# Scores of the middle stage from f16 halves instead of f32, with the context's halves kept in DRAM

## The chip, the core and the metric

The kernel runs on one core of one Trainium2 chip. A core has a matrix engine (PE, whose weight loads the profile shows apart as PEld), three engines for elementwise work (DVE, ACT and POOL), a sequencer that here only issues transfers (SP), and 16 DMA engines that move data between DRAM and on-chip memory. Each engine runs its own list of instructions in order, and engines wait for each other through semaphores. The metric is device microseconds (us) of one execution; less is better.

## What is computed

A small model over 32 batches: 112 query rows, 375 context rows, width 256. Cut to what matters:

```python
x = x + cross_attention_16_heads(ctx, layernorm(x))              # first stage
x = x + mixture_of_8_relu_experts(layernorm(x), counts_of_top2)  # first and middle stage
q = layernorm(x)                                                 # middle stage, "x2n"
logits = einsum('bqd,bkd->bqk', q, ctx) * 256**-0.5 + mask * -1e9
x = x + einsum('bqk,bkd->bqd', softmax(logits), ctx)
x = x + top2_of_8_experts(layernorm(x), W1, b1, W2, b2)          # routing in the middle stage, experts in the last
```

The change touches how `logits` is multiplied out.

## The kernel before

There are three stages, one after the other. The **first** (`attention_phase`, about the first half of the span) computes the 16-head attention batch by batch, with five batches in flight. For each batch SP loads the context transposed (`ctxT`, f32, 375 KB, line 244), ACT rounds it to f16 (`ctx_hi`, line 812), and POOL subtracts to get the rest (`ctx_lo`, f16, line 344). The key and value products then use three f16 products (high times high, high times low, low times high) in place of one f32 product. In the profile these tiles are all named `we`, since they lie in the memory of the later expert weights.

The **middle** stage (`middle_phase`) runs 39 steps. Step `u` works on several batches at once, as a pipeline with lags: the mixture of batch group `u` (`mixture`, 24 f16 matmuls of 448 columns, steps 0 to 31), the attention of batch `u-4` (called `a` in the code), its softmax and output (`o`, lag 5), the routing norm and logits (`r`, lag 6), and the choice of experts and scatter (`k`, lag 7). From step 7 on all parts are there; the mixture ends with step 31, and in steps 32 to 35 everything but the mixture runs. No scheduler orders this work: each engine has a function `step` in which its instructions stand in a written order, and semaphores do the rest. The lines that matter, by engine and in the order in which they stand in a step:

- PE: transposes of the mixture's sum (L1532), mixture parts 0 and 1 (L1516), transposes of `probs` (L1543), mixture part 2, the output product (L1551), transposes of `x2n` (L1557), mixture part 3, transposes of the routing row `rows` (L1564), two small rank products (L1575, L1576), **the scores** (L1582, two f32 products of 375 columns, each in two records), six route products (L1593).
- ACT: `probs` (L1621), `probsT` (L1626), `x2n` (L1632), `logit_exp` (L1636), `rows` (L1643), `w_hi` (L1649, the f16 rounding of a piece of the last stage's weights), `x2nT` (L1653), `xT_hi` (L1657).
- POOL: `ln_var`, `ln_rstd` and `ln_shift` for `x2n` (L1439, L1441, L1451), the same for `rows` (L1439, L1441, L1460), `mask_add` (L1466), `w_lo` (L1473, which waits for `w_hi` of the same step), a token number (L1480), and two scatters `dispatch_dram` (L1490, which wait for the slots that DVE writes on L1801).
- DVE: scores plus mask (L1713), norm statistics, four accumulations of the mixture (L1689, L1693), the choice of experts, `x3` (L1781, named `we` in the profile), `xT_lo` (L1788), rank pick and `slots_at` (L1797 to L1801).
- SP: a load of `w_raw`, of `ctxT` (f32 again, 375 KB, for the scores), of the mask and of `ctx_rows` per batch, and the store of `x3`.

The **last** stage (`expert_phase`) runs 35 tiles of 256 tokens through the chosen experts. It isn't touched.

Of the kernel before, what the change touches and what calls it, by code (L numbers as in the profile page):

```python
# [82 lines left out]
def attention_phase(nc, ctx, dram, keep):  # L83
# [14 lines left out]
    def within(cols, dt):  # L98
# [66 lines left out]
        x1n_ready x1lo_ready logits_ready choice_ready  # L165
# [67 lines left out]
    with nc.Block(no_gpsimd_drain=True) as block:  # L233

        @block.sync
        def _(sp):
            def load(t, u):
# [7 lines left out]
                             dram["ctxT"][bass.ds(b, 1), :, :].rearrange("o (c p) s -> p (o c) s", p=128)).then_inc(ctx_in[u % 2], 16)  # L245

# [19 lines left out]
            def step(t, u, on, more):  # L266
# [24 lines left out]
                if UNROLL <= t * UNROLL + u < B - 2:  # L291
                    load(t, u + 2)
                if a:
# [15 lines left out]
            for b in range(last - 2, last + 1):  # L309
# [18 lines left out]
        def _(pool):  # L328
# [467 lines left out]
        def _(act):  # L796
# [420 lines left out]
def middle_phase(nc, ctx, dram, keep):  # L1217
# [23 lines left out]
    ctxT = sb("ctxT2", [128, 2, DC, KV], F32)  # L1241
# [9 lines left out]
    x2nT = sb("x2nT", [128, DC, S], F32)  # L1251
# [20 lines left out]
    def reuse(*shape):  # L1272
# [42 lines left out]
    names = """weights_in bias_in share_ps share_rdy bias_rdy we_hi_rdy we_lo_rdy route_split consts  # L1315
        ctxT_in0 ctxT_in1 rows_in0 rows_in1 mask_in0 mask_in1 passed
        ffn_done accT_done x2nT_done s1_done pT_done o_done x3nT_done route_done
        x2nT_rdy exp_rdy pT_rdy x3hi_rdy lexp_rdy
        acc_rdy x2_rdy st2 ag2 x2n_rdy masked_rdy eb_rdy inv_rdy x3_rdy st3 ag3 x3n_rdy x3lo_rdy
        lg_rdy top_rdy at_rdy negtop_rdy pair_rdy sumw_rdy which_rdy comb_rdy chosen_rdy rank_done pick_rdy slots_rdy  # L1320
        cum_rdy token_rdy scattered0 scattered1 scattered2 scattered3 x3_out0 x3_out1 pads_out w_in0 w_in1 w_hi_rdy w_lo_rdy rows_set late_in tally_done table
# [42 lines left out]
    with nc.Block(no_gpsimd_drain=True) as block:  # L1364

        @block.sync
        def _(sp):
# [14 lines left out]
            for n in range(2):  # L1382
                sp.dma_start(dram["dispatch"][DUMMY + n * 128:DUMMY + (n + 1) * 128, :], dram["pads"][n]).then_inc(m["pads_out"], 16)
            for n in range(3):
                sp.dma_start(dram["out"][PAD_OUT + n * 128:PAD_OUT + (n + 1) * 128, :], dram["pads"][n][:, 0:D]).then_inc(m["pads_out"], 16)
# [7 lines left out]
            def load(t, u):  # L1393
# [6 lines left out]
                sp.dma_start(ctxT[:, p, :, :], dram["ctxT"][bass.ds(b, 1), :, :].rearrange("o (c p) s -> p (o c) s", p=128)).then_inc(ctxT_in[p], 16)  # L1400
# [20 lines left out]
            sp.wait_ge(m["pads_out"], 16 * 5)  # L1421
            sp.wait_ge(m["late_in"], 16 * len(keep["late_loads"]))
# [75 lines left out]
        def _(pe):  # L1498
# [4 lines left out]
            last.then_inc(m["share_ps"], 1)  # L1503
            pe.wait_ge(m["share_rdy"], 1)
# [16 lines left out]
            def step(t, u, on):  # L1521
# [38 lines left out]
                if r:  # L1560
                    wait(pe, m["x3n_rdy"], cnt(t, ur, 1, 1))
                    wait(pe, m["lg_rdy"], cnt(t, ur - 1, 1, 1))
                    for kc in range(DC):
                        last = nc.tensor.transpose(psum[:, 7, kc * S:(kc + 1) * S], rows[:, ur % ROW_SLOTS, kc * 128:(kc + 1) * 128], ident[0:S, 0:S])  # L1564
                    last.then_inc(m["x3nT_done"], 1)
                if k:
# [9 lines left out]
                    nc.tensor.matmul(rank, ones[:, 0:S], cum[:], start=False, stop=True).then_inc(m["rank_done"], 1)  # L1576
                if a:
# [3 lines left out]
                    for kc in range(DC):  # L1581
# [601 lines left out]
```

## Time and profile before

| | us |
|---|---|
| median of three runs (1086.59 to 1091.59) | 1090.93 |
| the profiled execution, its own time | 1090.87 |
| its span, first to last instruction | 1089.1 |
| PE busy in the span | 983.3 |
| DVE, POOL, ACT busy | 785.0, 560.8, 549.5 |
| middle stage, first mixture product to last scatter | 518.7 to about 844 |

A busy time is a sum over instructions. Matmul records overlap (each is drawn longer than the time to the next one's start), so a PE that looks busy all the time need not be what the others wait for. What a piece of work costs in a row of matmuls is read from start to start.

### The profile page before, as it was taken

How to read it: one execution, taken by the hardware profiler on the slowest of the kernel's cores; microseconds unless marked ns; L12 is line 12 of the kernel's file. 1: busy time of each engine (PE TensorE's matmuls, PEld its weight loads, DVE VectorE, ACT ScalarE, POOL GpSimd, SP SyncE). 2: the span in 40 equal slices, each digit the busy share in tenths (PEclk: the TensorE clock that was granted, in tenths of full speed). 3: DMA queues.
4: the chain of work that ended last, by engine and by line, in shares of the span. 5: the costliest groups of instructions: out<-in, count | busy, mean ns of one | idle time of the engine just before them, and what ended most of it. 6: DMA issues, size and time to landing. Idle time of an engine off the chain costs nothing. (4 is left out here: it accounts for less than half of the span.)

```text
span 1089.1 us, 31550 instructions
## 1 busy us (share of the span) xinstructions
PE 983.3 (90%) x10736; PEld 689.5 (63%) x10736; DVE 785.0 (72%) x2259; ACT 549.5 (50%) x1090; POOL 560.8 (51%) x839
## 2 busy tenths in 40 slices
PE   4699999999999999987999999999974599999993
PEld 3366666666666666655466666666643478888873
DVE  4578888888888888874768888888855256666653
ACT  3366666666666666653233344333432255555551
POOL 6545554555555555401146666666665245555444
PEclk9899999999999999987999999999987699999997
DMA  5444344443444444312545655565551345565543
GB/s 166 138 138 125 108 119 128 133 133 112 121 117 116 132 134 116 92 48 77 159 134 175 176 175 177 176 180 177 167 162 53 108 82 93 91 101 95 86 62 39
DMA packets 104589, 133.95 MB, mean 123 GB/s; under 512 B 23680, under 2 KB 93776, under 8 KB 104272
## 3 DMA queue, kind: packets, MB, share of 16 engines
q1 hardware_dynamic: 90898, 113.86, 36.2%
q0 software_dynamic: 13536, 18.10, 9.7%
q8 instruction: 89, 1.46, 0.6%
q14 instruction: 66, 0.54, 0.2%
HBM read 93.78 MB, written 38.68 MB: 122 GB/s over the span
## 5 line engine op out<-in xcount | busy, mean ns | idle before, releaser
L973 DVE TENSOR_REDUCE smax<-psum 112x2 f32<-112x750 f32 x240 | 221.3, 934 | 51.9 <-PE psum L425 48.8
L805 ACT ACTIVATE probsT<-psum 125x896 f32<-125x896 f32 x173 | 158.8, 918 | 59.2 <-PE psum L440 57.8
L1941 POOL DMA_INDIRECT out_dram<-y,token_at x70 | 110.8, 1583 | 117.3 <-DMA out_dram<-y,token_at 56.0
L2022 ACT ACTIVATE h<-psum,b 128x256 f32<-128x256 f32 x140 | 58.8, 471 | 105.6 <-PE psum L1969 105.6
L1490 POOL DMA_INDIRECT dispatch_dram<-rows,slots_at x64 | 64.2, 1003 | 45.7 <-DVE slots_at L1801 33.2
L1693 DVE SCALAR_TENSOR_TENSOR acc<-psum,neg_bias,acc 128x448 f32<-128x448 f32 x112 | 76.0, 680 | 11.8 <-PE psum L1516 11.6
L425 PE MATMUL psum<-k_stack,q_stack 63*128 63x375 f16 x480 | 79.0, 329 | 3.5 <-DVE smax L973 0.7
L460 PE MATMUL psum<-probsT,v_aug 125*32 125x112 f32 x2688 | 81.6, 262 | 0.0
L440 PE MATMUL psum<-q_stack,k_stack 64*128 64x112 f16 x1384 | 64.6, 213 | 11.9 <-DMA q_stack<-neg_max 7.7
L382 POOL CAST k_hi<-we 128x375 f16<-128x375 f32 x64 | 32.0, 500 | 79.0 <-ACT we L825 78.9
L1516 PE MATMUL psum<-xT_hi,we_hi 128*128 128x448 f16 x256 | 70.2, 356 | 1.9 <-DVE we_lo L1667 1.9
L1516 PE MATMUL psum<-xT_lo,we_hi 128*128 128x448 f16 x256 | 70.1, 356 | 0.0
L1516 PE MATMUL psum<-xT_hi,we_lo 128*128 128x448 f16 x256 | 69.9, 355 | 0.0
L440 PEld LDWEIGHTS psum<-q_stack,k_stack 64*128 64x128 f16 x1384 | 37.2, 95 | 50.6 <-ACT probsT L805 23.9
L460 PEld LDWEIGHTS psum<-probsT,v_aug 125*32 125x32 f32 x2688 | 61.6, 109 | 9.2 <-issue 4.8
L1969 PE MATMUL psum<-x_hi,w_hi 128*128 128x256 f16 x280 | 56.5, 284 | 11.0 <-DVE x_lo L2036 5.9
L493 PE MATMUL psum<-wv_hi,we 128*125 128x256 f16 x384 | 62.2, 285 | 1.5 <-ACT we L825 1.5
L384 POOL TENSOR_TENSOR k_lo<-we,k_hi 128x375 f16<-128x375 f32 x64 | 56.0, 876 | 5.1
L1621 ACT ACTIVATE probs<-probs,exp_bias 112x375 f32<-112x375 f32 x32 | 19.4, 607 | 77.1 <-DVE exp_bias L1716 77.1
L1969 PE MATMUL psum<-x_lo,w_hi 128*128 128x256 f16 x280 | 55.8, 283 | 0.0
L1969 PE MATMUL psum<-x_hi,w_lo 128*128 128x256 f16 x280 | 55.7, 282 | 0.0
L476 PE MATMUL psum<-we,wk_hi 128*128 128x375 f16 x256 | 53.4, 332 | 2.5 <-ACT we L825 1.1
(276 smaller groups left out, 2506.1 us busy)
## 6 DMA issues: line engine op xcount, KB each, us to landing
k_stack<-k_hi_dram SPq DMA_DIRECT2D x64, 188.0 KB, 2.9
we<-in_ctxT_dram SPq DMA_DIRECT2D x32, 375.0 KB, 3.8
ctxT<-in_ctxT_dram SPq DMA_DIRECT2D x32, 375.0 KB, 5.1
ctx_rows<-in_ctx_dram SPq DMA_DIRECT2D x32, 375.0 KB
rows_e<-dispatch_dram SPq DMA_DIRECT2D x70, 136.0 KB
w_raw<-in_w_dram SPq DMA_DIRECT2D x32, 256.0 KB, 4.2
k_hi_dram<-k_hi SPq DMA_DIRECT2D x32, 188.0 KB, 2.2
k_lo_dram<-k_lo SPq DMA_DIRECT2D x32, 188.0 KB, 2.1
```

The lines of the kernel that those rows point to most:

```text
L425: last = nc.tensor.matmul(psum[:, pair_bank(s) + a, 0:KV], queries(rows, b4, s, 128), keys_at(rows, b4, s, 0, KV), start=True, stop=True)
L440: last = nc.tensor.matmul(psum[:, a, r * S:(r + 1) * S], keys_at(rows, b4, 4 * hg + r, c * KC, 128), queries(rows, b4, 4 * hg + r, S), sta ...
L460: last = nc.tensor.matmul(bank_d[32 * j:32 * j + 32, g * S:(g + 1) * S], v_aug[:, b4d, cc, h, :], probsT[:, b2d, cc, h // 8, h % 2, h // 2 ...
L493: last = nc.tensor.matmul(bank[0:KC, n * D:(n + 1) * D], x[:, b2a, kc, cc * KC:(cc + 1) * KC], w[:, kc, :], start=(done == 0), stop=(done ...
L805: nc.scalar.activation(probsT[:, p, c, hg, :, :, :].rearrange("p k h q -> p k (h q)"), psum[0:KC, 0:2, 0:4 * S], ACT.Exp, scale=float(HD) ...
L973: nc.vector.reduce_max(smax[:, (u - LAG_B) % 2, 2 * (s % 4) + s // 4::PAIRS], psum[0:S, pair_bank(s):pair_bank(s) + 2, 0:KV], AX.X).then_i ...
L1490: nc.gpsimd.indirect_dma_start(dram["dispatch"], bass.IndirectOffsetOnAxis(slots_at[:, uk % ROW_SLOTS, n:n + 1], 0), rows[:, uk % ROW_SLOT ...
L1516: last = nc.tensor.matmul(psum[:, mix_bank(t, u, k), 0:GT], w[:, kc, e, hc * 128:(hc + 1) * 128], x[:, kc, bass.ds(g0, GT)], start=(n == 0 ...
L1693: nc.vector.scalar_tensor_tensor(out, psum[:, mix_bank(t, u, k), 0:GT], neg_bias[:, hc, e:e + 1], out, ALU.max, ALU.add).then_inc(m["acc_r ...
L1941: nc.gpsimd.indirect_dma_start(dram["out"], bass.IndirectOffsetOnAxis(token_at[:, n % 2, s:s + 1], 0), y[:, n % 2, s, :], None, compute_op ...
L1969: last = nc.tensor.matmul(psum[:, 1 + c // 2, (c % 2) * TILE:(c % 2 + 1) * TILE], w[:, bass.ds(e, 1), kc, c * 128:(c + 1) * 128].rearrange ...
L2022: nc.scalar.activation(h[:, c, :], psum[:, 1 + c // 2, (c % 2) * TILE:(c % 2 + 1) * TILE], ACT.Relu, bias=b1[:, c, bass.ds(e, 1)]).then_in ...
```

## The change

In the first stage, SP stores both halves of each batch's context to a new DRAM tensor `ctx_halves`, and ACT and POOL wait until a buffer's halves are out before they overwrite it. In the middle stage, SP reads these halves (f16, twice 187.5 KB) in place of the f32 `ctxT` (375 KB), and the scores become six f16 products (three pairs of halves, two chunks each) in place of two f32 ones. ACT writes the high half of the transposed `x2n`, DVE a new low half. Three orders change: on ACT `x2nT_hi` goes ahead of `rows`, and `w_hi` to the step's end; on PE the routing transposes go behind the rank products. Two pairs of semaphores are merged.

```diff
+            def halves_out(b):
+
+                for n, half_of in enumerate((ctx_hi, ctx_lo)):
+                    sp.dma_start(dram["ctx_halves"][b, n, :, :], half_of[:, b % 2, :, :].rearrange("p c k -> p (c k)")).then_inc(m["ctx_out"], 16)
...
+                if b >= 2:
+                    halves_out(b - 2)
...
+                if t * UNROLL + u >= B - 2:
+                    wait(sp, m["ctxlo_ready"], count(t, u, 1, 1))
+                    apart(sp)
+                    halves_out(t * UNROLL + u)
...
+            sp.wait_ge(m["ctx_out"], 32 * B)
...
                 wait(pool, m["v_done"], count(t, u - 2, 2, 2))
+                wait(pool, m["ctx_out"], count(t, u - 2, 32, 32))
                 nc.gpsimd.tensor_tensor(ctx_lo[:, u % 2, :, :], ctxT[:, u % 2, :, :], ctx_hi[:, u % 2, :, :], ALU.subtract).then_inc(m["ctxlo_ready"], 1)
...
                 wait(act, m["v_done"], count(t, u - 2, 2, 2))
+                wait(act, m["ctx_out"], count(t, u - 2, 32, 32))
                 nc.scalar.activation(ctx_hi[:, u % 2, :, :], ctxT[:, u % 2, :, :], ACT.Copy).then_inc(m["ctxhi_ready"], 1)
...
-                sp.dma_start(ctxT[:, p, :, :], dram["ctxT"][bass.ds(b, 1), :, :].rearrange("o (c p) s -> p (o c) s", p=128)).then_inc(ctxT_in[p], 16)
+                sp.dma_start(ctx_halves[:, p, :, :, :].rearrange("p n c k -> p n (c k)"),
+                             dram["ctx_halves"][b, :, :, :].rearrange("n p f -> p n f")).then_inc(ctxT_in[p], 16)
...
                 mix(3)
-                if r:
-                    wait(pe, m["x3n_rdy"], cnt(t, ur, 1, 1))
-                    wait(pe, m["lg_rdy"], cnt(t, ur - 1, 1, 1))
-                    for kc in range(DC):
-                        last = nc.tensor.transpose(psum[:, 7, kc * S:(kc + 1) * S], rows[:, ur % ROW_SLOTS, kc * 128:(kc + 1) * 128], ident[0:S, 0:S])
-                    last.then_inc(m["x3nT_done"], 1)
                 if k:
...
                     nc.tensor.matmul(rank, ones[:, 0:S], cum[:], start=False, stop=True).then_inc(m["rank_done"], 1)
+                if r:
+                    wait(pe, m["x3n_rdy"], cnt(t, ur, 1, 1))
+                    wait(pe, m["lg_rdy"], cnt(t, ur - 1, 1, 1))
+                    for kc in range(DC):
+                        last = nc.tensor.transpose(psum[:, 7, kc * S:(kc + 1) * S], rows[:, ur % ROW_SLOTS, kc * 128:(kc + 1) * 128], ident[0:S, 0:S])
+                    last.then_inc(m["x3nT_done"], 1)
                 if a:
                     wait(pe, ctxT_in[ua % 2], loads(t, ua))
                     wait(pe, m["x2nT_rdy"], cnt(t, ua, 1, 1))
                     wait(pe, m["masked_rdy"], cnt(t, ua - 1, 1, 1))
-                    for kc in range(DC):
-                        last = nc.tensor.matmul(psum[0:S, 4, 0:KV], x2nT[:, kc, :], ctxT[:, ua % 2, kc, :], start=(kc == 0), stop=(kc == DC - 1))
+                    n = 0
+                    for x, half_of in ((x2nT_hi, 0), (x2nT_hi, 1), (x2nT_lo, 0)):
+                        if n == 2 * DC:
+                            wait(pe, m["x2lo_rdy"], cnt(t, ua, 1, 1))
+                        for kc in range(DC):
+                            last = nc.tensor.matmul(psum[0:S, 4, 0:KV], x[:, kc, :], ctx_halves[:, ua % 2, half_of, kc, :], start=(n == 0), stop=(n == 5))
+                            n += 1
                     last.then_inc(m["s1_done"], 1)
...
+                if a:
+                    wait(dve, m["x2nT_rdy"], cnt(t, ua, 1, 1))
+                    nc.vector.tensor_tensor(x2nT_lo[:].rearrange("p c s -> p (c s)"), psum[:, 2, D:D + DC * S],
+                                            x2nT_hi[:].rearrange("p c s -> p (c s)"), ALU.subtract).then_inc(m["x2lo_rdy"], 1)
```

The order of ACT is easier to see as it stands in the two programs. A whole step of the middle stage on ACT, before (`rows` is the routing row, `w_hi` the rounded weights, `xT_hi` the high half of the transposed routing row):

```order
L1621 ACTIVATE probs,prob_sum<-probs,exp_bias 112x375
L1626 ACTIVATE probsT<-psum 125x336
L1632 ACTIVATE x2n<-x_res,ln_shift,ln_rstd 112x256
L1636 ACTIVATE logit_exp<-logits,neg_top 112x8
L1643 ACTIVATE rows<-we,ln_shift,ln_rstd 112x256
L1649 ACTIVATE w_hi<-w_raw 128x512
L1653 ACTIVATE x2nT<-psum 128x224
L1657 ACTIVATE xT_hi<-psum 128x2x112
```

`w_hi` stands directly behind `rows`. The same step on ACT in the changed kernel:

```order
L1640 ACTIVATE probs,prob_sum<-probs,exp_bias 112x375
L1645 ACTIVATE probsT<-psum 125x336
L1651 ACTIVATE x2n<-x_res,ln_shift,ln_rstd 112x256
L1655 ACTIVATE logit_exp<-logits,neg_top 112x8
L1659 ACTIVATE x2nT_hi<-psum 128x224
L1666 ACTIVATE rows<-we,ln_shift,ln_rstd 112x256
L1671 ACTIVATE xT_hi<-psum 128x2x112
L1676 ACTIVATE w_hi<-w_raw 128x512
```

`x2nT_hi` moved ahead of `rows`, and `w_hi` behind `xT_hi`. On PE, the end of a step before, from the transposes of `x2n` to the route products:

```order
L1557 MATMUL psum<-ident,x2n 128x112 x2
L1516 MATMUL psum<-xT_hi,we_hi 128x448 x2
L1516 MATMUL psum<-xT_lo,we_hi 128x448 x2
L1516 MATMUL psum<-xT_hi,we_lo 128x448 x2
L1564 MATMUL psum<-ident,rows 128x112 x2
L1575 MATMUL psum<-chosen,before 112x8
L1576 MATMUL psum<-cum,ones 112x8
L1582 MATMUL psum<-ctxT2,x2nT 112x375 x2
L1593 MATMUL psum<-route_whi,xT_hi 112x8 x2
```

The same place in the changed kernel:

```order
L1571 MATMUL psum<-ident,x2n 128x112 x2
L1530 MATMUL psum<-xT_hi,we_hi 128x448 x2
L1530 MATMUL psum<-xT_lo,we_hi 128x448 x2
L1530 MATMUL psum<-xT_hi,we_lo 128x448 x2
L1583 MATMUL psum<-chosen,before 112x8
L1584 MATMUL psum<-cum,ones 112x8
L1589 MATMUL psum<-ident,rows 128x112 x2
L1600 MATMUL psum<-ctx_halves,x2nT_hi 112x375 x4
L1600 MATMUL psum<-ctx_halves,x2nT_lo 112x375 x2
L1612 MATMUL psum<-route_whi,xT_hi 112x8 x2
```

The transposes of `rows` moved behind the two rank products, and the scores are six products. The order on POOL is the same in both.

## Rows read from the trace of the kernel before

**Rows 1.** Stretches of the span: us, busy us (instructions) per engine, granted clock, DMA.

```profile
core 0: us, PE busy (x) PEld busy (x) DVE busy (x) ACT busy (x) POOL busy (x), PEclk, DMA share, GB/s
...
570.00:780.00 210.00, 207.97 (x1241) 135.82 (x1242) 180.55 (x775) 82.48 (x210) 140.26 (x257) 1.00 0.59 175
```

**Rows 2.** Timeline, one steady step of the middle stage: start us, us, engine, line [idle].

```profile
659.54 1.49 PE L1582 MATMUL psum<-ctxT,x2nT 128*112 128x375 f32 x4
...
660.76 0.17 DVE L1801 CAST slots_at<-slots 112x2 uint32<-112x2 f32 x1
...
660.86 0.22 PE L1593 MATMUL psum<-route_whi,xT_hi 128*112 128x8 f16 x2
...
661.80 1.06 POOL L1490 DMA_INDIRECT dispatch_dram<-rows,slots_at  x1 [0.96 <-DVE slots_at L1801]
...
663.17 0.95 POOL L1490 DMA_INDIRECT dispatch_dram<-rows,slots_at  x1 [0.31 <-issue]
...
664.15 0.24 POOL L1439 TENSOR_SCALAR ln_var<-ln_mv 112x1 f32<-112x1 f32 x1
...
665.67 0.60 ACT L1632 ACTIVATE x2n<-x_res,ln_shift,ln_rstd 112x256 f32<-112x256 f32 x1 [1.04 <-POOL ln_shift L1451]
...
666.41 0.36 PE L1557 MATMUL psum<-ident,x2n 112*128 112x112 f32 x2
666.61 0.54 PE L1516 MATMUL psum<-xT_hi,we_hi 128*128 128x448 f16 x2
...
667.05 0.60 ACT L1643 ACTIVATE rows<-we,ln_shift,ln_rstd 112x256 f32<-112x256 f32 x1 [0.59 <-POOL ln_shift L1460]
...
667.55 0.61 ACT L1649 ACTIVATE w_hi<-w_raw 128x512 f16<-128x512 f32 x1
667.74 0.37 PE L1564 MATMUL psum<-ident,rows 112*128 112x112 f32 x2
...
667.95 0.27 PE L1575 MATMUL psum<-chosen,before 112*112 112x8 f32 x2
668.08 0.34 ACT L1653 ACTIVATE x2nT<-psum 128x224 f32<-128x224 f32 x1
668.08 0.34 PE L1576 MATMUL psum<-cum,ones 113*112 113x8 f32 x2
668.31 0.34 ACT L1657 ACTIVATE xT_hi<-psum 128x224 f16<-128x224 f32 x1
668.35 1.16 POOL L1473 TENSOR_TENSOR w_lo<-w_raw,w_hi 128x512 f16<-128x512 f32 x1 [0.86 <-ACT w_hi L1649]
668.51 1.17 PE L1582 MATMUL psum<-ctxT,x2nT 128*112 128x375 f32 x3
...
669.59 0.22 POOL L1480 TENSOR_SCALAR rows<-rows 112x1 f32<-112x1 f32 x1
```

**Rows 3.** Timeline, POOL, the last step with mixture products and the first without.

```profile
785.14 1.16 POOL L1473 TENSOR_TENSOR w_lo<-w_raw,w_hi 128x512 f16<-128x512 f32 x1 [0.86 <-ACT w_hi L1649]
...
794.10 1.16 POOL L1473 TENSOR_TENSOR w_lo<-w_raw,w_hi 128x512 f16<-128x512 f32 x1 [0.86 <-ACT w_hi L1649]
```

**Rows 4.** Timeline, PE in the first stage: six f16 products of 375 columns lie between.

```profile
224.67 0.82 PE L476 MATMUL psum<-we,wk_hi 128*128 128x375 f16 x4
...
225.64 0.35 PE L585 MATMUL psum<-ident,o_nat 112*128 112x112 f32 x2
```

**Rows 5.** Timeline, DVE and POOL in step 36, with no weights to split.

```profile
830.57 0.17 DVE L1801 CAST slots_at<-slots 112x2 uint32<-112x2 f32 x1
...
831.61 1.04 POOL L1490 DMA_INDIRECT dispatch_dram<-rows,slots_at  x1 [3.36 <-DVE slots_at L1801]
```

**Rows 6.** Timeline, a context load's issue and the next rounding (first stage).

```profile
224.79 0.42 SPq L244 DMA_DIRECT2D we<-in_ctxT_dram  x1
...
234.40 0.82 ACT L812 ACTIVATE we<-we 128x750 f16<-128x750 f32 x1
```

**Rows 7.** DMA issues: out<-in, engine, op, count, KB each, median us to landing.

```profile
k_hi_dram<-k_hi SPq DMA_DIRECT2D x32, 188.0 KB, 2.2
```

More of the change, by code:

```diff
@@ L1250, in middle_phase @@
     x2n = sb("x2n", [S, D], F32)
-    x2nT = sb("x2nT", [128, DC, S], F32)
+    x2nT_hi, x2nT_lo = sb("x2nT_hi", [128, DC, S], F16), sb("x2nT_lo", [128, DC, S], F16)
     probs = sb("probs", [S, KV], F32)
@@ L1313, in middle_phase @@
     second = sb("second", [S, E], F32)
[L1315 removed]
+    names = """weights_in bias_in share_rdy bias_rdy we_hi_rdy we_lo_rdy route_split consts
         ctxT_in0 ctxT_in1 rows_in0 rows_in1 mask_in0 mask_in1 passed
         ffn_done accT_done x2nT_done s1_done pT_done o_done x3nT_done route_done
[L1318 removed]
+        x2nT_rdy x2lo_rdy exp_rdy pT_rdy x3hi_rdy lexp_rdy
         acc_rdy x2_rdy st2 ag2 x2n_rdy masked_rdy eb_rdy inv_rdy x3_rdy st3 ag3 x3n_rdy x3lo_rdy
         lg_rdy top_rdy at_rdy negtop_rdy pair_rdy sumw_rdy which_rdy comb_rdy chosen_rdy rank_done pick_rdy slots_rdy
[L1321 removed]
+        cum_rdy token_rdy scattered0 scattered1 scattered2 scattered3 x3_out0 x3_out1 w_in0 w_in1 w_hi_rdy w_lo_rdy rows_set late_in tally_done table
         eps2 rs2 eps3 rs3 shift2 shift3 mask_rdy""".split()
@@ L1502, in _ @@
                 last = nc.tensor.matmul(psum[:, 0, 0:E], ones[0:S, :], gate_counts[:, n, :], start=(n == 0), stop=(n == 4))
-            last.then_inc(m["share_ps"], 1)
-            pe.wait_ge(m["share_rdy"], 1)
+            last.then_inc(m["share_rdy"], 1)
+            pe.wait_ge(m["share_rdy"], 2)
             def mixture(t, u, k):
@@ L1636, in step @@
                     nc.scalar.activation(logit_exp[:], logits[:], ACT.Exp, bias=neg_top[:]).then_inc(m["lexp_rdy"], 1)
+                if a:
+                    wait(act, m["x2nT_done"], cnt(t, ua, 1, 1))
+                    wait(act, m["s1_done"], cnt(t, ua - 1, 1, 1))
+                    nc.scalar.activation(x2nT_hi[:].rearrange("p c s -> p (c s)"), psum[:, 2, D:D + DC * S], ACT.Copy).then_inc(m["x2nT_rdy"], 1)
                 if r:
@@ L1644, in step @@
                                          scale=ln_rstd[:, 1, :]).then_inc(m["x3n_rdy"], 1)
+                if r:
+                    b0 = (t * TURN + ur) * S
+                    wait(act, m["x3nT_done"], cnt(t, ur, 1, 1))
+                    nc.scalar.activation(xT_hi[:, :, bass.ds(b0, S)], psum[:, 7, 0:DC * S].rearrange("p (c s) -> p c s", c=DC), ACT.Copy).then_inc(m["x3hi_rdy"], 1)
                 if a:
@@ L1649, in step @@
                     nc.scalar.activation(w_hi[:, bass.ds((t * TURN + ua) * W_PIECE, W_PIECE)], w_raw[:, ua % 2, :], ACT.Copy).then_inc(m["w_hi_rdy"], 1)
-                if a:
-                    wait(act, m["x2nT_done"], cnt(t, ua, 1, 1))
-                    wait(act, m["s1_done"], cnt(t, ua - 1, 1, 1))
-                    nc.scalar.activation(x2nT[:].rearrange("p c s -> p (c s)"), psum[:, 2, D:D + DC * S], ACT.Copy).then_inc(m["x2nT_rdy"], 1)
-                if r:
-                    b0 = (t * TURN + ur) * S
-                    wait(act, m["x3nT_done"], cnt(t, ur, 1, 1))
-                    nc.scalar.activation(xT_hi[:, :, bass.ds(b0, S)], psum[:, 7, 0:DC * S].rearrange("p (c s) -> p c s", c=DC), ACT.Copy).then_inc(m["x3hi_rdy"], 1)
             steps(act, step)
```

19 lines of the change are left out of this document (10 added, 9 removed).

## The prediction, made before the changed kernel was run

> **What bounds the kernel now.** I read the busy times by stretch first. From 570 to 780 us, the steady part of the middle stage, PE is busy 207.97 of 210 us at the full granted clock (1.00, the 2.4 GHz level) [rows 1]. That looks like a stage bound by PE, and the change makes PE's scores cheaper. So I then read one step line by line, and looked for a start that waits for nothing but PE.
>
> The step's period is 668.51 - 659.54 = 8.97 us, from one start of the scores to the next [rows 2]. Follow the idle notes backwards. `x2n` on ACT waited 1.04 us for POOL's `ln_shift`. `rows` on ACT (667.05) waited 0.59 us for POOL's second `ln_shift`. `w_hi` (667.55) runs straight behind `rows`. POOL sat idle for 0.86 us and started `w_lo` (668.35) when `w_hi` was done; then come the token (669.59), and the scatters, the first of which starts 8.97 us after the last step's at 661.80, hence at about 670.77. Behind the two scatters POOL starts `ln_var` (664.15 in the row) with no wait, and that leads to the next `x2n`, 1.52 us later, and the next `rows` 1.38 us after that. This is a closed ring: scatter, `ln_var`, `rows`, `w_hi`, `w_lo`, token, scatter. Its pieces: scatter to `ln_var` 664.15 - 661.80 = 2.35; `ln_var` to `rows` 667.05 - 664.15 = 2.90; `rows` to `w_lo` 1.30; `w_lo` to token 1.24; token's start to scatter 1.18. Sum 8.97: the whole period, with no slack [rows 2].
>
> The test of this reading is the place where the mixture's products stop. With them PE loses 24 products a step (four parts of 667.74 - 666.61 = 1.13 us, about 4.5 us [rows 2]). `w_lo` of the last step with mixture starts at 785.14, that of the first without at 794.10: 8.96 us, unchanged [rows 3]. **The ring through POOL and ACT sets the pace, not PE**, though PE fits in it with little to spare.
>
> A second ring shares most of this: `rows` to PE's transposes to `xT_hi` to DVE's `slots_at` to the scatter. `slots_at` ends at 660.93, the token at 660.62 + 0.22 = 660.84 [rows 2]. So the slots are last by 0.09 us, and the two rings are nearly equal.
>
> **The change, part by part.**
>
> *Scores on PE.* Two f32 products take 660.86 - 659.54 = 1.32 us [rows 2]. Six f16 products of 375 columns take 225.64 - 224.67 = 0.97 us [rows 4]. Saved: 0.35 us a step. The scores also wait today for `x2nT` (668.08 + 0.34 = 668.42, behind `w_hi` on ACT), while the rank products were issued at 667.95 and 668.08: a gap of 0.43 where the spacing is 0.13, about 0.27 us of it a wait [rows 2]. With `x2nT_hi` ahead of `rows` that goes too. PE's own work becomes 8.97 - 0.62 = 8.35 us a step. This is worth time only where PE is the bound. In steps 4 to 6, which have no scatter, I take 3 x 0.35 = 1.1 us as a gain. In the others it is slack.
>
> Here a rule can be weighed against the trace. By busy share PE leads with 99% of the stretch [rows 1], and yet the period doesn't move when half of its work goes [rows 3]. The Trainium skill (Perfetto Trace Analysis, Identifying the Most-Contended Engine) says to take the engine with the highest occupancy as the most contended one and to optimize it first, and warns in the same place that matmul busy time is a poor measure for PE. By the first half of that rule this edit gains all its 0.62 us a step; by the rows it gains nothing in a full step. The measurement is with the warning.
>
> *`x2nT_lo` on DVE.* The nearest row is ACT's rounding of the same 128x224 from PSUM, 0.34 us [rows 2]; DVE is busy 180.55 of 210 us [rows 1], 7.7 us of a period, and 8.1 with it. It fits under any period above 8.4, and it stands ahead of `xT_lo`, which will wait for ACT anyway. I cost it at nothing.
>
> *`w_hi` moved behind `xT_hi`.* This is the costly part. POOL's list is unchanged: `w_lo`, token, scatters, then the next step's norms. So whatever delays `w_hi` delays the next `x2n`. Today `w_hi` needs only `rows`. Now it needs `xT_hi`, which needs PE's transposes of `rows`, and these stand behind mixture part 3 and the rank products, which stand behind the transposes of `x2n`. The ring becomes (from the end of `x2n`, all from [rows 2]):
>
> - to PE's transposes of `x2n`: 666.41 - 666.27 = 0.14; PE was busy then, and will not be, so 0.05 to 0.14;
> - transposes 0.20, mixture part 3 1.13, first rank product 0.13, second one 0.13 (0.1 to 0.25, its end is hidden today), transposes of `rows` 0.37: 1.96;
> - to `xT_hi` about 0.05; `xT_hi` to `w_hi` 0.23 (as from 668.08 to 668.31 on ACT); `w_hi` 0.61; to `w_lo` 668.35 - 668.16 = 0.19: 1.08;
> - `w_lo` to the token's start 1.24, the token 0.22: 1.46;
> - token to scatter: not shown with the token last. The scatter starts 0.87 us after `slots_at` ends; in step 36 it is 831.61 - 830.74 = 0.87 again [rows 5], so this counts from the last thing waited for. From POOL's own instruction the signal comes sooner (`w_lo`'s end to the token 0.08, ACT's `w_hi` to `w_lo` 0.19), so 0.87 - 0.11 = 0.76. Bounds: 0.31, the gap before the second scatter, and 0.87;
> - scatter to `ln_var` 2.35, `ln_var` to `x2n` 1.52, `x2n` 0.60: 4.47.
>
> Sum 0.10 + 1.96 + 1.08 + 1.46 + 0.76 + 4.47 = **9.83 us**, against 8.97: +0.86 a step. Bounds: 9.3 (0.31 for the scatter, short ends) to 10.1. PE then needs only 8.35 of 9.83 us and waits for `x2n` about 1.5 us a step. The slots' ring gets shorter: `xT_hi` starts 0.15 us sooner after `rows`, so it can't be the bound.
>
> The new ring closes once for each step that has both a scatter and mixture part 3: steps 7 to 31, 25 times: 25 x 0.86 = 21.5 us. Steps 32 to 35 have no mixture; there the transposes wait for `rows` (1.38 + 0.60 after the start of `x2n`), then 0.37 + 0.05 + 0.23 + 0.61 + 0.19 + 1.46 + 0.76 + 3.87 us and 0.09 to start: 9.6, +0.65, four times: 2.6 us.
>
> *Stores and waits in the first stage.* 64 issues of about 0.4 us on SP, each 188 KB, as `k_hi_dram`'s, which land in 2.2 us [rows 7]. They are issued behind the load at 224.79, and the wait for them is in the next step's rounding, at 234.40 [rows 6]: 9.2 us of room for about 1 us of issue, the load ahead of them and some 5 us of transfers. Behind the stores SP has the query reloads, used two steps later. Behind ACT's new wait stand `oT` and the exponentials, and for these PE waits; so a late store would cost at once, but I see none late. Cost 0, with up to 3 us for more DMA traffic. Reading two f16 halves moves as many bytes as the f32 load. The last stage is the same.
>
> **Sum**, against the profiled execution's own time of 1090.87 us (0.06 below the median of the three runs, which I ignore): 1090.9 + 21.5 + 2.6 - 1.1 + 0 = **1113.9, say 1114 us**, 2.1% slower.
>
> **The rivals.**
>
> *PE is the bound after all* (faster). All 28 steps with scores and mixture gain 0.62 us: 1090.9 - 17.4 = 1073.5 us. For it: PE's 99% [rows 1]. Against it: the unchanged 8.96 us without mixture [rows 3], and idle notes that name POOL. It decides only if POOL could start the next norms before its scatters, which its written order excludes. Above it stands the rule of the Trainium skill cited on the most contended engine. Chance 0.07.
>
> *`w_lo` has slack that I don't see* (about the same or a little faster). If the token's branch took at most the slots' time, the slots' ring would be left, 0.15 us shorter: 1090.9 - 25 x 0.15 - 1.1 = 1086 us. For it: today slots and token end within 0.09 us of each other, so one may hide the other. Against it: `w_hi` starts 1.1 us later in the step, ten times that. Chance 0.05.
>
> *The stores hurt the first stage as well* (slower still). If they hold back `neg_max` or the rounding by 0.5 us in each of 28 steps, add 14: 1128 us. It decides from a landing more than about 9 us after the load's issue. Against it: landings of 2.2 us [rows 6, 7]. Chance 0.06.
>
> **How the numbers follow.** The forecast has the remaining 0.82. Its own range comes from the ring: 25 x 0.35 + 1 - 1 = +9 to 25 x 1.15 + 3.5 + 3 - 1 = +34. Taking the ends as unlikely together, 1100 to 1122 us holds it nearly always, and the other cases stay outside: about 8 in 10. A measurement of this kernel can tell about 0.5% from no change, 5.5 us. Faster: the first rival and half of the second, 0.10; the same: 0.05; slower: 0.85.
>
> **What would show it.** In the new profile: the scores' period in steady steps 9.8 us (9.3 to 10.1); `w_lo` starting right behind a `w_hi` that starts right behind `xT_hi`; PE idle before the transposes of `x2n`, released by ACT; six score products in 0.97 us; the first scatter 0.76 us behind the token, with `slots_at` done long before. A first stage of the same length shows the stores hidden. The prediction is wrong if the period is 8.9 or less, or if ACT's rounding of the context names a DMA as what it waited for.

## The result: 2.4% slower, and the profile after

The changed kernel takes 1117.18 us (median of four runs, 1115.72 to 1120.04) against 1091.26 us before. One of the four runs before took 2346.79 us and stands in that median; without it the median is 1090.93. The ratio is 1.0239, 95% interval 1.0211 to 1.0266. The prediction was 1114 us, 1100 to 1122.

The profiled execution took 1120.04 us, its span is 1118.2 us, so 29.1 more than the 1089.1 of before. Two marks that stand in both programs split the difference. The last rounding of a context in the first stage starts at 447.41 (before 440.62). The first `w_lo` of the middle stage starts at 551.70 (before 544.45) and the last at 850.63 (before 821.73). So the first stage lost 6.8 us, the stretch from first to last `w_lo` 21.65 us, and the rest 0.7 us. The last stage gave and took nothing.

The stretch that answers to [rows 1], from the view of stretches:

```profile
core 0: us, PE busy (x) PEld busy (x) DVE busy (x) ACT busy (x) POOL busy (x), PEclk, DMA share, GB/s
...
570.00:780.00 210.00, 189.95 (x1184) 123.47 (x1182) 184.63 (x734) 79.81 (x194) 129.33 (x238) 1.00 0.52 162
```

PE was busy 207.97 of 210 us and is now busy 189.95, at the same granted clock (1.00). It waits. The view of waits for the same stretch says for whom (engine, line, what it waited for; us in all, times, longest):

```profile
POOL w_lo L1487 <- ACT w_hi L1676: 43.1, 21, 3.0
...
PE psum L1571 <- ACT x2n L1651: 20.1, 21, 1.3
```

That is 0.96 us a step at the transposes of `x2n`, which is where the forecast put PE's wait, at about 1.5 us. One steady step of the timeline, to be read beside [rows 2] (start us, us, engine, line, and in brackets the idle time before):

```profile
664.87 1.16 POOL L1487 TENSOR_TENSOR w_lo<-w_raw,w_hi 128x512 f16<-128x512 f32 x1 [2.01 <-ACT w_hi L1676]
...
666.91 1.06 POOL L1504 DMA_INDIRECT dispatch_dram<-rows,slots_at  x1 [0.59 <-issue]
...
669.26 0.24 POOL L1453 TENSOR_SCALAR ln_var<-ln_mv 112x1 f32<-112x1 f32 x1
...
670.78 0.60 ACT L1651 ACTIVATE x2n<-x_res,ln_shift,ln_rstd 112x256 f32<-112x256 f32 x1 [2.24 <-POOL ln_shift L1465]
...
671.43 0.41 PE L1571 MATMUL psum<-ident,x2n 112*128 112x112 f32 x2 [0.94 <-ACT x2n L1651]
...
672.70 0.38 DVE L1803 TENSOR_TENSOR x2nT_lo<-psum,x2nT_hi 128x224 f16<-128x224 f32 x1
...
673.37 0.81 PE L1600 MATMUL psum<-ctx_halves,x2nT_hi 128*112 128x375 f16 x4
673.57 0.36 ACT L1671 ACTIVATE xT_hi<-psum 128x224 f16<-128x224 f32 x1 [0.80 <-PE psum L1589]
673.82 0.62 ACT L1676 ACTIVATE w_hi<-w_raw 128x512 f16<-128x512 f32 x1
...
674.63 1.16 POOL L1487 TENSOR_TENSOR w_lo<-w_raw,w_hi 128x512 f16<-128x512 f32 x1 [2.01 <-ACT w_hi L1676]
...
674.69 1.12 DVE L1824 CAST slots_at<-slots 112x2 uint32<-112x2 f32 x1
...
675.87 0.22 POOL L1494 TENSOR_SCALAR rows<-rows 112x1 f32<-112x1 f32 x1
...
676.68 1.06 POOL L1504 DMA_INDIRECT dispatch_dram<-rows,slots_at  x1 [0.59 <-issue]
```

The period is 674.63 - 664.87 = 9.76 us (before 8.97). `w_hi` starts right behind `xT_hi`, `w_lo` 0.19 us behind `w_hi`, and the scatter comes last. One row was not forecast at all: `slots_at`, a copy of two numbers per row that took 0.17 us before [rows 2], now takes 1.12 us. It starts 0.06 us behind `w_lo` and ends at 675.81, 0.02 us behind it. The experiments show that this is what closes the ring.

### The profile page after: what moved, and what is told of

The parts are those of the page before. It is cut to its first block and busy times, and to the rows that moved or that the text cites. A ratio compares the mean times of both kernels' runs of the same rounds, so it can differ in the third digit from the quotient of the medians.

```text
span 1118.2 us, 31777 instructions
## 1 busy us (share of the span) xinstructions
PE 986.2 (88%) x10800; PEld 692.8 (62%) x10800; DVE 811.7 (73%) x2291; ACT 553.9 (50%) x1090; POOL 561.2 (50%) x839
## 5 line engine op out<-in xcount | busy, mean ns | idle before, releaser
L1487 POOL TENSOR_TENSOR w_lo<-w_raw,w_hi 128x512 f16<-128x512 f32 x32 | 37.1, 1158 | 65.5 <-ACT w_hi L1676 65.5
L1651 ACT ACTIVATE x2n<-x_res,ln_shift,ln_rstd 112x256 f32<-112x256 f32 x32 | 19.2, 600 | 85.2 <-POOL ln_shift L1465 85.1
## 6 DMA issues: line engine op xcount, KB each, us to landing
ctx_halves_dram<-we SPq DMA_DIRECT2D x64, 187.5 KB, 4.3
```

## The experiments

All periods below are from start to start of `w_lo` in steady steps. Where a ratio is given, its runs stand beside runs of the kernel before on the same chip. Edits are shown short; `+` is added, `-` taken out.

### Is it the place of w_hi?

The kernel before with only `w_hi` moved (on ACT):

```diff
 rows
-w_hi
 x2nT
 xT_hi
+w_hi
```

> The kernel before, with one edit: on ACT, w_hi goes behind xT_hi, the last of the step. f32 scores, no stores of halves, PE's order as before. If the ring through w_hi and POOL sets the pace, the period of the middle stage's steps rises from 8.96 us although nothing else has changed. From the end of x2n: x2nT on PE 0.05 + 0.20, mixture part 3 1.13, transposes of rows 0.37, to xT_hi 0.05, w_hi 0.23 + 0.61, w_lo 0.19 + 1.16, then 0.87 (scatter) and 4.47 to the next x2n: about 9.4 us, so 25 x 0.4 = 10 us more, 1101 us. If the new form of the scores costs the time (the rival), or if w_hi has slack on ACT, the period stays 8.96 us and the time 1091 us.

Measured: 1104.93 us, ratio 1.0132 [1.0114, 1.0151], period 9.43 to 9.47. With f32 scores, no stores and no other order touched, the one move costs 14 us. `slots_at` takes 1.12 us here too, 0.05 to 0.07 us behind the start of `w_lo`. The changed kernel's 9.76 lies 0.3 us higher still. The two rank products that it puts ahead of the transposes of `rows` take 673.14 - 672.82 = 0.32 us from start to start, but no run moves them alone.

The changed kernel with only `w_hi` moved back behind `rows`:

```diff
 x2nT_hi
 rows
+w_hi
 xT_hi
-w_hi
```

> The changed kernel, with one edit: on ACT, w_hi goes back to directly behind rows, ahead of xT_hi. The ring theory: w_lo starts about 1.3 us after rows again and the period falls from 9.76 to 9.0 us; what is left over 8.96 is the rank products that now stand ahead of the transposes of rows. 27 x 0.7 = 19 us less than the changed kernel, about 1098 us; the first stage keeps its longer start. If the six products or the low half on DVE set the pace, the period stays 9.76 us and the time 1117 us.

Measured: 1096.96 us, ratio 1.0061 [1.0043, 1.0079], period 8.94 to 9.03. It takes back 20 of the 26 us. `w_hi`'s place is shown from both sides.

### All three orders of before, with f16 scores

```diff
 (ACT) rows, w_hi, x2nT_hi, xT_hi      (was: x2nT_hi, rows, xT_hi, w_hi)
 (PE)  transposes of rows ahead of the rank products
```

> The changed kernel with all three orders of the kernel before (rows, w_hi, x2nT_hi, xT_hi on ACT; transposes of rows ahead of the rank products on PE): it differs from the kernel before by the f16 scores, the low half on DVE and the stores and loads of halves alone. The ring theory: the period is 8.96 us, to 0.05, since PE's cheaper scores lie beside the ring; the middle stage is as long as before and the time is that of the kernel before plus what the first stage lost, 1091 + 3 to 7 = 1094 to 1098 us. If PE were a bound, the period would fall to about 8.6 us and the time to 1085 us. If the form of the scores cost time, the period would be above 9.2 us.

Measured: 1099.45 us, ratio 1.0078 [1.0054, 1.0102], period 9.27 to 9.35 in the steps with mixture and 8.94 to 8.97 at the end. That is a miss: I had expected 8.96 throughout, since I had costed `x2nT_lo` on DVE at nothing. Its DVE rows in a step (timeline) show the price:

```profile
676.92 0.39 DVE L1803 TENSOR_TENSOR x2nT_lo<-psum,x2nT_hi 128x224 f16<-128x224 f32 x1 [0.99 <-ACT x2nT_hi L1672]
...
677.23 0.68 DVE L1712 SCALAR_TENSOR_TENSOR acc<-psum,neg_bias,acc 128x448 f32<-128x448 f32 x1
...
677.82 0.38 DVE L1811 TENSOR_TENSOR xT_lo<-psum,xT_hi 128x224 f16<-128x224 f32 x1
...
678.54 0.17 DVE L1824 CAST slots_at<-slots 112x2 uint32<-112x2 f32 x1
```

With `w_hi` ahead of `x2nT_hi`, DVE waits 0.99 us for ACT, and the last accumulation of the mixture, `xT_lo` and the slots all stand behind that wait. Without mixture there is no accumulation in between, and the period is the old one. So the new DVE instruction costs 0.35 us a step unless `x2nT_hi` is early: the reorder on ACT was needed, but only of `x2nT_hi`, not of `w_hi`. (The kernel of the edit before, with `x2nT_hi` early, differs from this one in PE's order too; that it is DVE's row and not PE's is read from the rows above, where DVE runs without a pause from `x2nT_lo` to the slots.)

### What does the scatter wait for?

The prediction closed the ring with the token number. The kernels of this part are the changed kernel with small edits; they tell the token from the held `slots_at`. In the first, `w_lo` works on 8 of its 512 columns (the low halves of the last stage's weights are zero, so that part of the computation is left out).

```diff
-w_lo[:, at : at + 512] = w_raw - w_hi
+w_lo[:, at : at + 8] = w_raw - w_hi
```

> The changed kernel with w_lo cut to 8 of its 512 columns; the rest of the tile is set to zero once at the start of the middle stage, so the low halves of the last stage's weights are left out of the computation. In the changed kernel slots_at, a copy of 112x2 on DVE, is recorded with 1.12 us in a steady step and ends with w_lo (675.81 against 675.79), where it took 0.17 before. Theory (DVE's small copy is held while POOL's w_lo runs): slots_at takes 0.17 us again, the first scatter comes 0.87 us behind the later of slots_at's end and about 0.1 us of POOL's own wait, and the ring loses w_lo's 1.16 us less what a tiny w_lo and the slots leave: 9.76 - 0.9 = about 8.8 us, which is at PE's own 8.4 to 8.8. Rival (slots_at is long because it waits in its own queue for its input, and w_lo has slack): slots_at still takes over 1 us and the period stays at 9.7.

Measured: 1091.42 us (one run beside 1091.08, the median of the kernel before), period 8.79 to 8.81 in most steps.

```profile
664.62 0.21 POOL L1488 TENSOR_TENSOR w_lo<-w_raw,w_hi 128x8 f16<-128x8 f32 x1 [2.04 <-ACT w_hi L1677]
...
664.82 0.17 DVE L1825 CAST slots_at<-slots 112x2 uint32<-112x2 f32 x1
...
665.87 1.06 POOL L1505 DMA_INDIRECT dispatch_dram<-rows,slots_at  x1 [0.73 <-issue]
```

`slots_at` is back at 0.17 us, and the scatter starts 665.87 - 664.99 = 0.88 us behind its end. Since this kernel shortens `w_lo` as well, it doesn't say by itself which link closes the ring. The next three leave the work as it is. The first moves two small things on DVE, so that `slots_at` starts ahead of `w_lo`:

```diff
+combine weights (rows<-unscaled,first_w)
 xT_lo
-combine weights (rows<-unscaled,first_w)
 slots (two picks)
-cum
 slots_at
+cum
```

> The changed kernel with two small moves on DVE: the combine weights (rows<-unscaled,first_w) ahead of xT_lo, where DVE waits for ACT anyway, and cum behind slots_at. slots_at then starts some 0.15 to 0.25 us sooner, just ahead of w_lo, where it started 0.06 us behind it. Theory (a copy that starts while POOL's w_lo runs is held to its end, and the scatter starts 0.87 us behind the later of what it waits for; the token's own link to the scatter is shorter than what the changed kernel shows): slots_at takes 0.17 us again, the scatter starts 0.31 us behind the token's end, and the period falls from 9.76 by 0.59 - 0.31 to 9.48 us, about 1109 us in all. Rival (the scatter follows the token by 0.59 to 0.76 us whatever slots_at does, as the prediction had it): the period stays at 9.76 us, 1117 us in all.

The second moves the token number ahead of `w_lo` on POOL:

```diff
 mask_add
+token
 w_lo
-token
 two scatters
```

> The changed kernel with the token number ahead of w_lo on POOL and nothing else. w_lo still waits for w_hi, so it starts at the same place, and the scatter stands directly behind it. Theory (the held slots_at is the last thing that the scatter waits for): slots_at still ends with w_lo, the scatter starts 0.87 us behind that, the period stays at 9.76 us, 1117 us in all. Rival (the token is the last link, as the prediction had it): the scatter follows the end of w_lo by 0.31 us, the period falls by 0.08 + 0.22 + 0.59 - 0.31 = 0.58 to 9.18 us, about 1101 us in all.

> Both moves together: slots_at sooner on DVE and the token ahead of w_lo on POOL. Theory (held slots_at, then POOL's own order): neither the copy nor the token is behind w_lo any more, the scatter follows w_lo's end by 0.31 us, the period falls to 9.18 us, about 1101 us in all. If slots_at is still held, it stays at 9.76 as with the token's move alone. If the token's link alone counted, it would be as fast as the kernel with the token's move alone.

Measured, one run each: 1103.07 us with the slots sooner (period 9.36 to 9.47), 1119.13 us with the token first (9.76 to 9.78), 1099.11 us with both (9.06 to 9.11); the kernel before took 1091.56 beside them. A step of the first, with the slots sooner:

```profile
668.89 0.17 DVE L1824 CAST slots_at<-slots 112x2 uint32<-112x2 f32 x1
...
668.97 1.19 POOL L1487 TENSOR_TENSOR w_lo<-w_raw,w_hi 128x512 f16<-128x512 f32 x1 [2.03 <-ACT w_hi L1676]
...
670.24 0.22 POOL L1494 TENSOR_SCALAR rows<-rows 112x1 f32<-112x1 f32 x1
...
670.63 1.06 POOL L1504 DMA_INDIRECT dispatch_dram<-rows,slots_at  x1 [0.17 <-issue]
```

And of the second, with the token first:

```profile
664.15 1.16 POOL L1494 TENSOR_TENSOR w_lo<-w_raw,w_hi 128x512 f16<-128x512 f32 x1 [1.68 <-ACT w_hi L1676]
...
664.21 1.12 DVE L1824 CAST slots_at<-slots 112x2 uint32<-112x2 f32 x1
...
666.21 1.06 POOL L1504 DMA_INDIRECT dispatch_dram<-rows,slots_at  x1 [0.89 <-DVE slots_at L1824]
```

Taking the token off the path gives nothing, since the copy is still held. Letting the copy start 0.08 us ahead of `w_lo`, where it started 0.06 us behind it, gives 0.37 us a step, some 10 of the 14 us that this run lies below the changed kernel's median (the runs stand on different chips, and the rest isn't explained). Together they give 0.66 a step; the scatter then follows the end of `w_lo` by 668.70 - 668.52 = 0.18 us:

```profile
667.34 1.18 POOL L1494 TENSOR_TENSOR w_lo<-w_raw,w_hi 128x512 f16<-128x512 f32 x1 [1.71 <-ACT w_hi L1676]
...
668.70 1.06 POOL L1504 DMA_INDIRECT dispatch_dram<-rows,slots_at  x1 [0.18 <-issue]
```

So in the changed kernel the last link is: end of `w_lo`, end of the held `slots_at`, 0.87 us, scatter. From the token's end to the scatter it takes only 670.63 - 670.46 = 0.17 us (the kernel with the slots sooner).

The Trainium skill (SBUF — State Buffer, SBUF: two separate sides) describes this: GpSimd (POOL) and VectorE (DVE) share one pair of ports to on-chip memory, which is an exclusive lock for the length of an instruction. By its text the lock matters for DVE work in a two-port mode, or with two inputs from on-chip memory while POOL's instruction reads that memory too, and whichever starts first has it. Here "on-chip memory" leaves out PSUM, the memory that PE writes its results to. The traces agree in what they show. Held beside POOL's `w_lo` are the copy `slots_at` (1.12 us for 0.17), the combine weights (0.54 for 0.22 in the kernel before) and the small product `unscaled` (about 1.5 for 0.16, below). Never held are the accumulations (0.68), `xT_lo` (0.38) and `x2nT_lo` (0.38), which all read PSUM. Nor is `exp_bias`, one number per row that reads no PSUM (0.15 beside `w_lo` in every kernel where the two meet). No run here shows which mode an instruction ran in.

### The first stage's stores

In steps 1 to 3 of the first stage, SP issues the stores of the halves ahead of the queries' stores. This kernel puts them behind:

```diff
-halves_out(b - 2)          (steps 1 to 3, with b = u + 2)
 store q_hi, q_lo
+halves_out(u)              (steps 1 to 3)
```

> The changed kernel with one edit in the first stage: in steps 1 to 3 SP issues the stores of halves behind the stores of q_hi and q_lo, not ahead of them. Theory: of the 6.8 us that the first stage is longer, about 2.4 us come from the clock's later rise in that execution and 4.4 us from queries' stores that lie behind 375 KB more in the DMA queues, so that SP, waiting for them, sends neg_max late. With the edit the 4.4 us go: about 1113 us. If the loss is DMA traffic as such, wherever it is issued, the time stays 1117 us.

Measured: 1110.93 us, ratio 1.0203 [1.0168, 1.0239], period unchanged (9.75). The median is 6.2 us below the changed kernel's, on another chip, and the two intervals of the ratio overlap, so the times alone don't show a gain. The place of the last rounding does, over all 14 profiles of this study. It starts at 440.62 to 443.28 us (mean 442.0) in the four kernels without stores, at 444.56 to 447.41 (mean 446.2) in the seven with the stores ahead of the queries, and at 441.19 to 443.05 (mean 442.1) in the three with the stores behind them. So the order on SP costs about 4 us, and with the stores behind the queries nothing of it is left. SP's rows in the changed kernel (timeline):

```profile
52.61 0.94 SPq L240 DMA_DIRECT2D ctx_halves_dram<-we  x2
...
54.15 0.46 SPq L193 DMA_DIRECT2D q_lo_dram<-q_lo  x1
...
60.34 1.10 SPq L198 DMA_DIRECT2D q_stack<-q_hi_dram  x2
...
63.29 2.32 SPq L282 DMA_DIRECT2D q_stack<-neg_max  x2
...
66.89 0.37 PE L453 MATMUL psum<-q_stack,k_stack 64*128 64x112 f16 x8 [2.17 <-DMA q_stack<-neg_max]
```

And with the stores behind the queries:

```profile
50.15 0.36 SPq L193 DMA_DIRECT2D q_lo_dram<-q_lo  x1
...
50.56 0.99 SPq L240 DMA_DIRECT2D ctx_halves_dram<-we  x2
...
54.49 1.10 SPq L198 DMA_DIRECT2D q_stack<-q_hi_dram  x2
...
59.37 1.41 SPq L282 DMA_DIRECT2D q_stack<-neg_max  x2
...
62.67 0.37 PE L455 MATMUL psum<-q_stack,k_stack 64*128 64x112 f16 x8
```

The reload of the queries comes 60.34 - 54.15 = 6.2 us behind the last of their stores when the context's stores stand ahead of it, and 54.49 - 50.15 = 4.3 us behind it otherwise. The maxima behind it on SP are then late too, and PE waits 2.17 us for them. The view of transfers gives the stores' landing (out<-in, engine, operation, count, KB each, median us to landing):

```profile
ctx_halves_dram<-we SPq DMA_DIRECT2D x64, 187.5 KB, 4.3
...
k_hi_dram<-k_hi SPq DMA_DIRECT2D x32, 188.0 KB, 2.8
```

They land in 4.3 us, not the 2.2 of `k_hi_dram` before [rows 7], and that one grew to 2.8. ACT's rounding waits for a store once:

```profile
44.01 0.83 ACT L826 ACTIVATE we<-we 128x750 f16<-128x750 f32 x1 [2.11 <-DMA ctx_halves_dram<-we]
```

That wait is there with the stores behind the queries as well (42.51, 2.39 us, and 0.53 us at 30.34). The view of waits counts no other in the changed kernel, and the steady distance between roundings is 14.72 us in both kernels.

About 2 us of the 6.8 are no part of the change. The third rounding starts at 20.94 us in the profile of before and at 23.35 in that of after. It goes with the moment at which PE's products get twice as fast. In the profiles of before and of the changed kernel, four key products each (before, then after):

```profile
14.77 0.81 PE L476 MATMUL psum<-we,wk_hi 128*128 128x375 f16 x4 [0.57 <-ACT we L825]
...
14.79 1.44 PE L489 MATMUL psum<-we,wk_hi 128*128 128x375 f16 x4 [0.57 <-ACT we L839]
```

Over the 14 profiles, products are fast from this place on in two, before and the kernel with `w_hi` back behind `rows` and the stores in place (third rounding at 20.94 and 20.96 us). In ten they get fast at 17 to 19 us (21.48 to 22.39), among them the other three kernels without stores. In two, the changed kernel and one of the next section, they are slow until 20 us (23.35 and 23.72). So it doesn't follow the edits. The expectation above puts it down to the clock; the view of stretches gives a granted clock of 1.00 from 10 to 25 us in both profiles, so that isn't shown.

### Can both be had: w_hi early

If `w_hi`'s place sets the ring, ahead of `x2n` is better than either, since ACT waits for POOL there anyway. With that, the transposes of `rows` ahead of the rank products, and the stores behind the queries:

```diff
 probsT
+w_hi
 x2n
 logit_exp
 x2nT_hi
 rows
 xT_hi
-w_hi
```

> The changed kernel with w_hi put between probsT and x2n on ACT, the transposes of rows back ahead of the rank products on PE, and the first stage's stores behind the queries' stores. w_hi then runs where ACT waits for POOL's ln_shift anyway (1.04 us of idle before x2n in the kernel before), so w_lo can start behind the second ln_shift, and the ring through rows, xT_hi and the slots is what is left. Theory (the ring is set by w_hi's place): the period falls to 8.5 us, with PE's own 8.35 to 8.5 just under it: 25 x 0.45 = 11 us under the kernel before, and about +1 for the first stage: 1080 us, ratio 0.99. Rival (the period is bound by DVE or PE at 8.9 whatever w_hi's place is): 1090 us, ratio 1.00.

The kernel before with only `w_hi` moved there (f32 scores, no stores):

> The kernel before with nothing changed but w_hi put between probsT and x2n on ACT. The f32 scores remain, so PE's own work stays at about 8.7 to 8.9 us a step. Theory: the ring through w_hi falls below PE, and PE sets the pace: period 8.7 to 8.8 us, 25 x 0.2 = 5 us less, 1085 us. In the steps without mixture PE is not the bound, and the period falls to 8.5 or less. If this kernel is as fast as the one with f16 scores, the f16 scores are worth nothing even with w_hi out of the way; the difference of the two is what they are worth. Rival (the ring through w_hi was not the bound before): period 8.96, 1090.5 us.

Measured: 1088.19 us, ratio 0.997 [0.9949, 0.9992], with f16 scores, and 1097.79 us, ratio 1.0068 [1.0044, 1.0093], with f32 scores. Both missed. In both the short steps have 8.48 us, which is what I expected of the first (for the second I had expected PE to hold them at 8.7 to 8.8). But some steps are long: three of 10.1 to 10.4 us in the steady part of the first, every other one of 9.8 in the second. A long step of the first (timeline):

```profile
658.14 0.52 POOL L1482 TENSOR_SCALAR mask_add<-mask 112x375 f32<-112x375 f32 x1
...
658.28 1.53 DVE L1786 CUSTOM_DVE_ANT_0 unscaled<-logit_exp,chosen 112x8 f32<-112x8 f32 x1
...
658.64 1.15 POOL L1489 TENSOR_TENSOR w_lo<-w_raw,w_hi 128x512 f16<-128x512 f32 x1
```

The hold again, now of another small product, through two POOL operations back to back. It takes 0.16 us in the short steps. The next two kernels put `unscaled` and the two reciprocals behind it ahead of DVE's third accumulation, so that they are done before `mask_add`:

```diff
 chosen
+unscaled, inv_sum, first_w
 acc (third of four)
-unscaled, inv_sum, first_w
 x3
```

> The kernel with w_hi ahead of x2n and f16 scores had a period of 8.48 us in most steps, but about 10.1 in four of them: there DVE's small product unscaled (0.16 us alone) was recorded with 1.5 us, from POOL's mask_add to the end of w_lo. This kernel puts unscaled and the two reciprocals ahead of DVE's third accumulation of the mixture, so they are done before mask_add starts. Theory (small DVE work with both inputs in on-chip memory is held while POOL's tensor operations run, work that reads PE's results is not): no long step is left, all periods 8.5 us, about 4 x 1.7 = 7 us less: 1081 us. Rival (the long steps come from something else that then holds unscaled): the long steps stay, 1088 us.

> The same move of unscaled and the two reciprocals in the kernel before with w_hi ahead of x2n, so with the f32 scores and no stores in the first stage. There every other step was long (9.8 us against 8.48, 11 of 22 with unscaled at 1.2 to 1.6 us). Theory: all periods 8.48 us, set by the ring through rows, xT_hi and the slots, with PE's f32 scores still below it; 25 x 0.49 = 12 us less than the kernel before: 1079 us. It would be as fast as the one with f16 scores, which then are worth nothing here. Rival (PE is the bound at 8.5 to 8.9 us with f32 scores): 1085 us or more, and the f16 kernel ahead by 4 us.

Measured: 1086.98 us, ratio 0.9966 [0.994, 0.9991], with f16 scores; 1088.60 us, ratio 0.9972 [0.9952, 0.9991], with f32 scores. With f16 scores no `unscaled` is held any more in the steady steps, and the longest steady step has 9.10 us. But the short ones became 8.5 to 8.9, so only 1.2 us came of it, not 7 (the runs of each of the two spread over 8 to 10 us). With f32 scores two were still held (1.54 us), 9.2 us came back, and the period is mostly 8.73. Neither reached the 1079 to 1081 that I expected.

With f32 scores the traces show what holds the steps: PE, the rival of that expectation. From 590 to 650 us, the first line with f32 scores, the second with f16 scores (columns as in the view of stretches above):

```profile
590.00:650.00 60.00, 60.00 (x366) 40.21 (x365) 50.38 (x226) 25.06 (x63) 40.94 (x75) 1.00 0.62 182
...
590.00:650.00 60.00, 59.94 (x385) 40.05 (x383) 52.31 (x239) 26.06 (x63) 41.94 (x77) 1.00 0.63 182
```

A busy share of 100% says little by itself. But with f32 scores each start on PE follows the one before at the distance that it has in the other kernels, with no wait in a step, and the transposes of `x2n` come every 8.73 us:

```profile
641.57 0.36 PE L1557 MATMUL psum<-ident,x2n 112*128 112x112 f32 x2
...
650.30 0.36 PE L1557 MATMUL psum<-ident,x2n 112*128 112x112 f32 x2
```

So PE's own work in a step with f32 scores is 8.73 us, only 0.23 under the ring of the kernel before. With f16 scores the scores take 649.52 - 648.52 = 1.00 us from start to start in place of 644.75 - 643.42 = 1.33, which makes PE's own work an estimated 8.40 us. The transposes of `x2n` come every 8.60 to 8.68 us in most steps, so PE isn't the whole bound there, and what is I haven't separated.

Both kernels with the weights first are a little faster than the kernel before, by 0.3%, and 1.6 us apart with ranges that overlap (1083.46 to 1093.63 and 1086.33 to 1091.05). So with everything else put right, f16 scores are worth at most a fraction of a per cent here: they save 0.33 us of PE work a step, of which the period shows about 0.1.

## Why the prediction was right, and where not

**What bounds the kernel.** Right in what mattered: PE at 99% was not the pace. Its scores got cheaper (six products in 674.41 - 673.37 = 1.04 us, forecast 0.97), nothing was gained, and it now stands idle for 20 of 210 us. But it was close: once the ring was shortened, PE's f32 work bounded the step at 8.73 us. The caution in the Trainium skill (Perfetto Trace Analysis, Identifying the Most-Contended Engine), that matmul busy time doesn't tell how near PE is to its limit, is borne out: PE was busy for 207.97 of 210 us, and its work still wasn't what set the period.

**The ring through `w_hi`.** Forecast 9.83 us, measured 9.76. Term by term: from the end of `x2n` to `xT_hi` 2.11 forecast, 673.57 - 671.38 = 2.19 measured; `xT_hi` to `w_lo` 1.03 and 1.06; `w_lo` to the end of the token 1.46 and 1.46; token to scatter 0.76 and 0.59; scatter to the end of `x2n` 4.47 and 4.47.

**The last link.** Here the step "token to scatter" failed in its mechanism, not only in its size. The token's own price is 0.17 us, below my lower bound of 0.31. What takes the 0.59 is `slots_at`, which I expected "done long before", held until `w_lo` ends and then 0.87 us from the scatter. Had the copy not been held, the period would have been 9.4 (that kernel measured 9.36 to 9.47), still in my range. The number was right partly because what I had put together behind `w_lo`'s end (0.08, 0.22 and 0.76, 1.06 us) is near to the 0.89 that the held copy takes.

The same corrects my reading of the kernel before. I read two rings that were equal by chance within 0.09 us. In fact DVE's combine weights were held by `w_lo` there too, and `slots_at` stood behind them:

```profile
669.00 0.54 DVE L1793 TENSOR_SCALAR rows<-unscaled,first_w 112x8 f32<-112x8 f32 x1
```

They take 0.22 us where no `w_lo` runs beside them, and here they end at 669.54, 0.03 us behind `w_lo` (668.35 + 1.16). So `w_lo` was on the path before as well, by way of DVE and not of the token. This is read from the rows; no run takes this hold alone out of the kernel before.

**The count.** Forecast 25 x 0.86 + 4 x 0.65 - 1.1 = 23.0 us in the middle stage. From first to last `w_lo` it was 21.65: 22 steps by 0.79 = 17.4, the last six together 4.0, the first three 0.3. The four distances that end in steps without mixture are 9.87, 9.86, 9.85 and 9.45 us, where I had 9.6, and in the kernel before one of them was already 9.71; so they added 2.4 us. The gain of 1.1 us in steps 4 to 6 didn't come.

**`x2nT_lo` on DVE at nothing.** Right in this kernel, but for a reason that I hadn't given: only since `x2nT_hi` is early on ACT. With the old order it costs 0.35 us a step.

**The first stage at nothing, up to 3.** Wrong. It lost 6.8 us in the profiled execution, about 4 of them by the change, all through the order on SP. The term that I had at nothing is SP's order in steps 1 to 3: I looked for the wait in the steady steps, where indeed there is none, but not in those, where the queries' stores stand behind the context's. That the stores land in 4.3 us instead of 2.2 costs little by itself: with the stores behind the queries they still take 4.1, and the first stage is as long as without them. The sign that I had set for a miss, a rounding that names a DMA, shows once, at 44.01.

**Rivals.** "PE is the bound" and "`w_lo` has slack" are excluded by the period. "The stores hurt the first stage" was right in kind and much too large in size (about 4 us from the first steps, not 14 from 28). The ring came out 1.4 us cheaper than forecast and the first stage dearer by more, so part of the agreement in the total is two errors that cancel. The median rose by 26.2 us (from 1090.93) where I had 23.

## What to carry to other kernels

Before moving an instruction on one engine, follow who waits for it on the others, until the path comes back to the same instruction one step later: here one 0.6 us rounding, moved 1.1 us later, cost 20 us. An engine that is 99% busy in the profile isn't shown to be the bound until a stretch with less work for it gets shorter. And look at the durations of the smallest instructions: one that takes 1.1 us in one place and 0.17 in another is held by someone, and a move of a tenth of a microsecond can free it.

## What the runs showed of the hardware

Beside a POOL tensor operation of 1.16 us, small DVE instructions that read and write on-chip memory other than PSUM can be held to its end: 1.12 us for 0.17, 0.54 for 0.22, 1.53 for 0.16 (this one through two POOL operations back to back). It depends on which starts first: started 0.08 us ahead of `w_lo`, the copy took 0.17 us. Not all are held: `exp_bias`, 112x1, took 0.15 us beside `w_lo`, and in the kernel with the slots sooner, `cum`, with both inputs in on-chip memory, started in the same hundredth as `w_lo` and took 0.16 us, and `w_lo` took 1.19 instead of 1.16.

A scatter through indices starts 0.87 to 0.89 us behind the end of the DVE copy that writes them, wherever that copy is the last thing it waits for. It starts only 0.17 to 0.18 us behind POOL's own instruction when the copy ended 1.2 us or more ahead of the scatter (the kernels with the slots sooner).

The stores of 187.5 KB, issued behind a load of 375 KB, landed in 4.3 us, where stores of 188 KB had landed in 2.2 before. Whether the load ahead or the added traffic does it wasn't separated.
